# Routing in two expert layers: one-hot rows built by three tensor_tensor operations for eight tiles instead of sixteen tensor_scalar operations

## The reference, cut to what matters

```python
x = x + attn_a(layernorm(x))       # gated delta-rule scan
x = x + ffn(layernorm(x))          # experts, first layer
x = x + attn_b(layernorm(x))       # low-rank attention
x = x + ffn(layernorm(x))          # experts, second layer

def ffn(x):                        # 8 experts, top 2, d_ff 512
    gate_logits = xs @ Wg                               # 8192 x 8
    weights, sel = top_k(gate_logits, 2); weights = softmax(weights)
    h = relu(einsum('td,edf->etf', xs, W1) + b1)        # only the chosen experts count
    out_e = einsum('etf,efd->etd', h, W2) + b2
    out = sum over the 2 chosen experts of weights * out_e[sel]
```

## Time and profile before

| | before |
|---|---|
| median of 3 runs | 2487.86 us (2483.36 to 2488.05) |
| profiled execution, its own time | 2479.44 us |
| its span, first to last instruction | 2477.7 us |
| mean granted TensorE clock | 0.813 |
| busy: PE, DVE, ACT, POOL | 69%, 77%, 58%, 57% |
| inversion, first call (L1359/L1360 stretch) | 854.10 to 907.93 us |
| inversion, second call | 1986.61 to 2040.45 us |

### The profile page before, as it was taken

How to read it: one execution, slowest core, us unless ns; L and a number is a source line. 1 busy time by engine, 2 the same in 40 slices (tenths; PEclk the granted TensorE clock), 3 DMA queues, 4 the chain that set the end, 5 groups by cost and what they waited for, 6 DMA issues and landing times. The chain is left out here.

```text
span 2477.7 us, 59443 instructions
## 1 busy us (share of the span) xinstructions
PE 1701.6 (69%) x16780; PEld 1378.8 (56%) x16781; DVE 1907.8 (77%) x4981; ACT 1442.7 (58%) x3723; POOL 1401.4 (57%) x1511
## 2 busy tenths in 40 slices
PE   3666575766643459995688888888885656777671
PEld 1545454443533429994477777777774625565550
DVE  5999899899946878884699889888993795445446
ACT  3666566666632238884388778777784235444440
POOL 2545445454540017773488888888874007777771
PEclk8778787777765559997799999999997558889985
DMA  1000001010024103333122111122113201111127
GB/s 27 11 16 17 23 13 26 14 26 13 22 64 124 38 9 89 90 89 57 31 54 54 49 48 53 51 53 54 48 42 86 64 0 46 50 50 50 49 50 216
DMA packets 186756, 122.01 MB, mean 49 GB/s; under 512 B 23937, under 2 KB 175393, under 8 KB 186529
## 3 DMA queue, kind: packets, MB, share of 16 engines
q1 hardware_dynamic: 149632, 69.94, 10.6%
q0 software_dynamic: 17920, 36.74, 6.1%
q10 hardware_dynamic: 18976, 12.59, 1.7%
HBM read 66.22 MB, written 44.04 MB: 44 GB/s over the span
## 5 line engine op out<-in xcount | busy, mean ns | idle before, releaser
L1814 POOL TENSOR_TENSOR att_pl<-att_p,att_ph 128x384 f16<-128x384 f32 x512 | 462.3, 919 | 114.8 <-ACT att_ph L2034 104.1
L1039 POOL DMA_INDIRECT ffn_xs<-normed,ffn_tokeni x288 | 305.9, 1062 | 386.9 <-DVE posi L1390 148.7
L325 POOL TENSOR_TENSOR sq<-states,qS 128x256 f32<-128x256 f32 x256 | 243.1, 949 | 332.2 <-DVE states L726 310.2
L538 ACT ACTIVATE decayed<-states,alpha 128x64 f32<-128x64 f32 x1024 | 272.2, 336 | 197.2 <-DVE states L726 195.7
L1223 ACT ACTIVATE ffn_h<-bank,b_cols 128x256 f32<-128x256 f32 x576 | 227.6, 475 | 178.5 <-PE bank L1133 176.2
L381 PE MATMUL bank<-sq,ident 128*128 128x128 f32 x1024 | 249.9, 415 | 104.2 <-POOL sq L325 104.2
L2031 ACT ACTIVATE att_p<-bank 128x384 f32<-128x384 f32 x512 | 252.4, 493 | 106.0 <-PE bank L1908 101.5
L2128 DVE TENSOR_REDUCE att_mx<-bank 128x3 f32<-128x384 f32 x512 | 277.6, 551 | 47.2 <-PE bank L1875 42.1
L381 PEld LDWEIGHTS bank<-sq,ident 128*128 128x128 f32 x1024 | 219.8, 239 | 137.2 <-POOL sq L325 111.4
L2034 ACT ACTIVATE att_ph<-bank 128x384 f16<-128x384 f32 x512 | 252.1, 492 | 0.0
L1146 PE MATMUL bank<-w_h,ffn_hh 128*128 x1152 | 231.3, 231 | 2.1 <-DVE ffn_hl L1414 1.7
(11 more groups left out here) (337 smaller groups left out, 5167.1 us busy)
## 6 DMA issues: line engine op xcount, KB each, us to landing
slots<-ffn_ys SPq DMA_DIRECT2D x72, 128.0 KB
ffn_x_all<-x SPq DMA_DIRECT2D x16, 512.0 KB, 7.2
normed<-ffn_xn ACTq DMA_DIRECT2D x32, 256.0 KB, 2.3
att_qz<-att_qp SPq DMA_DIRECT2D x256, 32.0 KB, 1.9
ffn_yg<-picked SPq DMA_DIRECT2D x32, 256.0 KB, 4.6
ffn_xs<-normed,ffn_tokeni POOLq DMA_INDIRECT x288
xin<-in_x SPq DMA_DIRECT2D x64, 64.0 KB, 1.9
xres<-in_x SPq DMA_DIRECT2D x64, 64.0 KB, 2.0
```

The lines of the kernel that those rows point to most:

```text
L325: nc.gpsimd.tensor_tensor(sq[:, t, :].rearrange("p (h i j) -> p h i j", h=HL, i=D), states[:, t, :].rearrange("p (h i j) -> p h i j", h=HL ...
L538: ins = nc.scalar.activation(decayed[:, 64 * h:64 * h + 64], states[:, (t - 1) % TC, 64 * h:64 * h + 64], ACT.Copy, scale=alpha[p][:, t, h ...
L1039: pool.indirect_dma_start(xs[j % AHEAD][:, r, :], None, A["normed"], bass.IndirectOffsetOnAxis(ap=tokeni[:, BR * j + r:BR * j + r + 1], ax ...
L1814: nc.gpsimd.tensor_tensor(pl[:, h % RP, :], p32[:, h % RP, :], ph[:, h % RP, :], ALU.subtract).then_inc(low_done, 1)
```

## The change

One function, `onehot`, builds the rows of the eight columns of a group with three operations in place of sixteen. The single value per partition becomes a broadcast operand: `tile_of` and `col_of` are read as [128, 8, 144] and [128, 8, 128] with the last dimension repeated, and the constant rows are repeated over the eight columns. The multiplication by `nth`, which was the second half of the `tensor_scalar` on `isa`, becomes an operation of its own, in place on `isa`. A new semaphore `matched` holds it until the comparison has been written. `nth` and `col` become float16, and one copy per call makes `tile16`, a float16 copy of `tile`.

```diff
-        self.nth = sb("nth", [P, 2 * NT])
+        self.nth = sb("nth", [P, 2 * NT], F16)
...
-        pos, tile, col = (sb(n, [P, 2, NT]) for n in ("pos", "tile", "col"))
+        pos, tile = (sb(n, [P, 2, NT]) for n in ("pos", "tile"))
+        col, tile16 = (sb(n, [P, 2, NT], F16) for n in ("col", "tile16"))
...
-        onehots, rowed, counted = (sem(n) for n in ("onehots", "rowed", "counted"))
+        matched, onehots, rowed, counted = (sem(n) for n in ("matched", "onehots", "rowed", "counted"))
...
-            tile_of, col_of = (x[:, :, :].rearrange("p k t -> p (k t)") for x in (tile, col))
+            did("tile16", v.tensor_copy(tile16[:, :, :], tile[:, :, :]))
+            tile_of, col_of = (x[:, :, :].rearrange("p k t -> p (k t)") for x in (tile16, col))
...
-                for q in range(TQ):
-                    at = bass.ds(u * TQ + q, 1)
-                    v.tensor_scalar(isb[p][:, q, :], X.slot_col[:, :], col_of[:, at], None, ALU.is_equal)
-                    ins = v.tensor_scalar(isa[p][:, q, 0, :], X.slot_tile[:, :], tile_of[:, at], X.nth[:, at],
-                                          ALU.is_equal, ALU.mult)
+                at = bass.ds(u * TQ, TQ)
+                v.tensor_tensor(isa[p][:, :, 0, :], X.slot_tile[:, :].unsqueeze(1).to_broadcast([P, TQ, NA]),
+                                tile_of[:, at].unsqueeze(2).to_broadcast([P, TQ, NA]), ALU.is_equal).then_inc(matched, 1)
+                v.tensor_tensor(isb[p][:, :, :], X.slot_col[:, :].unsqueeze(1).to_broadcast([P, TQ, P]),
+                                col_of[:, at].unsqueeze(2).to_broadcast([P, TQ, P]), ALU.is_equal)
+                dve.wait_ge(matched, u + 1)
+                ins = v.tensor_tensor(isa[p][:, :, 0, :], isa[p][:, :, 0, :],
+                                      X.nth[:, at].unsqueeze(2).to_broadcast([P, TQ, NA]), ALU.mult)
                 ins.then_inc(onehots, 1)
```

More of the change, by code:

```diff
@@ L865 @@
          "base", "cend", "cnt", "over", "nb", "bend", "bstart", "adj", "slot", "p1", "pos1", "p2", "pos2",
-         "tile0", "tile1", "tile", "col", "past", "blk", "blki", "den", "w1", "w2",
+         "tile0", "tile1", "tile", "col", "tile16", "past", "blk", "blki", "den", "w1", "w2",
          "sums_kept", "one", "inverse", "row0", "row1", "row", "held", "id0", "id", "id_held", "second", "token0", "token"]
```

## The result

The changed kernel took 2497.21 us (median of 10 runs, 2494.28 to 2507.64). The kernel before now has ten runs as well, with a median of 2482.89 us (2474.41 to 2488.05). The ratio is 1.0064, with a 95% interval of 1.0047 to 1.0080, which is 11.7 to 19.9 us slower, 15.9 us in the middle; the two medians are 14.3 us apart. The forecast was 2499 us, and slower.

A forecast was written before the change was run, and what follows sets the result against it. DVE's groups and the wait for two buffers were taken to bound both exposed inversions. Losses of 5.6 us a call, 11.2 in both, plus 0.5 for `tile16` gave +11.7 on 2487.86, stated as 2499 us; range 2489 to 2512.

The forecast's parts named there:

- The path: Both inversions, one per call: nothing runs beside them, so any gain or loss reaches the kernel's end twice.
- The cost of the sixteen: DVE's sixteen old operations per group: 0.60 us of columns, 1.25 of fixed cost, 1.32 of scalars, together 3.17 us.
- The pace of the three: The three new DVE operations: 1.043 ns per column for all 3328 columns, 3.71 us a group.
- the first rival: New DVE operations take two columns at a time: 1.97 us a group, kernel 20.1 us faster, 2467.8 us; chance 0.09.
- The waits: DVE's wait for `matched` is met behind `isb`'s comparison and costs nothing; DVE runs without a pause.
- The 0.02 us to spare: Margin hiding the return trip in the inversion: two buffers give 7.40 us per two groups, DVE alone 7.42.
- G: DVE's time for one group, start to start, in the inversion: 3.13 us before, forecast 3.71 us.
- The rival without overlap: Long DVE operations don't overlap: 4.04 us a group, 22.3 us slower in all, 2510 us; chance 0.10.
- The limit before: In the old inversion two buffers hold two groups to 6.82 us, where DVE alone would give 6.26.
- the return trip: From a group's last DVE operation through ACT's copy and PE's 8 matmuls until DVE gets the release: 3.61 us.
- The sum: Whole kernel: 5.6 us lost a call, 11.2 in both, plus 0.5 for `tile16`; +11.7 us, forecast 2499 us.
- the base: Time of the kernel before to which the loss was added: the median of the runs shown, 2487.86 us.

The follow-up runs named there:

- e3: Kernel before with only `isb` built by one comparison, `isa` still by eight `tensor_scalar`; ratio 1.0003 to the kernel before, inversion 52.7 us.
- e4: Changed kernel with `isb` again built by eight `tensor_scalar`, `isa` still by comparison and multiplication; ratio 1.0056 to the kernel before, inversion 62.0 us.
- e7: Changed kernel with the eight columns stored innermost in `isa`, `isb` and the constant rows, on a slower chip; ratio 1.0091 to the kernel before there.
- e9: Changed kernel with each repeated value stored twice side by side and the operations walking in twos; ratio 0.9915 to the kernel before, inversion 42.0 us.
- e11: Changed kernel with the multiplication directly behind `isa`'s comparison and `isb`'s comparison last, so the wait is open; ratio 1.0086 to the kernel before.
- e6: Kernel before with four buffers of `isa` and `isb` in place of two, on a slower chip; ratio 1.0003 to the kernel before there.
- e12: Kernel before with four buffers of `isa` and `isb`, run once more on the faster kind of chip; ratio 1.0014 to the kernel before.
- e10: e9 with four buffers of `isa` and `isb` in place of two; ratio 0.9886 to the kernel before, inversion 32.0 us.
- run 32: Not a follow-up run or kernel: the words belong to "PE had run 32 matmuls without a break", said of e10.
- e8: e7 with four buffers of `isa` and `isb`, on the slower chip; ratio 1.0138 to the kernel before there, inversion 55.5 us.

## Why the prediction was right

**The path.** Both inversions lie in the open: right. POOL's first fetch moved from 2049.72 to 2059.64, and nothing took it back.

**The cost of the sixteen.** The split into columns, fixed part and scalar reads gave 3.17 for a measured 3.13 us. e3 and e4 recombine the same prices: e3 came out as expected (1.4 us a call), e4 0.5 us under it (7.9 for 8.4).

**The pace of the three.** This was the step with the widest bounds, 0.26 to 1.043 ns per column, and the choice of L1316 as the nearest row was right: forecast 1.36, 1.23 and 1.36 us, measured 1.354, 1.217 and 1.350. The reason given, that the repeated value is itself the stream, is borne out by e7 and e9: with another order of the same elements, or with each value stored twice, the pace doubles. So the first rival had its size right (0.76 and 0.69) and only its condition not met. The rule of the Trainium skill, "Vector Engine (DVE) Microarchitecture Reference", section 5.1, that the mode with two results per cycle wants an innermost step of one and that one repeated element runs at one per cycle, agrees with this case on both sides: 1354 ns with the repeated element innermost, 759 with a row.

**The waits.** `matched` costs nothing in the place where it stands (starts 1.14 us apart), and DVE no longer waits for PE. The 0.02 us to spare was in the forecast G: with the measured 3.68 the two limits are 7.36 and 7.38 us a pair, closer than the rows can tell, and the rows show 7.36. The rival without overlap is refuted by the changed kernel's own rows. e11 shows what the wait would cost if it were open.

**The limit before.** That the two buffers and the return trip, and not DVE, set the pace before is shown by e6 and e12, 50.3 and 50.2 us against 54.2.

**The sum.** Forecast 59.5 us to the end of group 15, which is 59.4 to the first step behind it; measured 58.8. G was 3.68 in place of 3.71, and the small pauses of the loop that I had put in did not occur. With `tile16` that is 10.5 us against the forecast 11.7. The measured ratio is 15.9 us, and its interval begins at 11.7. So the sum is right, to 1.2 us, for what the trace locates, and the total is larger by a part that stays open. That the predicted time is within 2 us of the measured one is partly luck: the base, 2487.86, was 5.0 us above the median of ten runs, and the difference 2.6 us too small by the medians (11.7 for 14.3) and 4.2 by the ratio.

## What to carry to other kernels

Count what the operations stream before counting the operations: 16 short ones with a scalar went at nearly four columns per 1.04 ns, and the three long ones with a repeated value at one, so a saving of 2.3 us a group in fixed costs and scalar reads was paid for with 2.9 us of columns. If a repeated value has to be a tensor operand, store it twice side by side and walk in twos; in e9, with float16 throughout, this doubled the pace without touching what other engines read; no run tried it with float32. And read the loss or gain of a loop from its return trip: before the change the buffers and not DVE set the pace, which made the loss smaller than 16 x 0.55 us, and nearly halved the gain in e9's inversions until there were four buffers.

## What the runs showed of the hardware that I had not expected

- The moving operand of a matmul read with a stride of 16 bytes in float16 halves TensorE's pace at a clock of 0.50 (e7: 0.52 us a matmul of 288 columns against 0.24, the seven steps of a group's 2.10 us less its last 0.45). The weight load with the same stride is no slower (medians 146 and 151 ns).
- An open wait between two long DVE operations costs 0.13 us in unrolled code and 0.21 us in a hardware loop (e11).
- The granted clock in the inversion was 0.86 on the mean in e10, after PE had run 32 matmuls without a break, and a group of 8 matmuls fell from 2.10 to 1.15 us. So a faster DVE was paid twice. In e8 PE ran 66 us without a break and the clock stayed at 0.50; the reason is open.
- All four traces of kernels with four buffers in the expert layers have an attention stage 8 to 17 us longer, on both kinds of chip, although no instruction of it was edited. PE's "issue" time in it is 21.6 to 23.6 us against 15.7 to 17.5. The cause is open.
